# Local attention scores as one wave of 64-row tiles on keys written four times, with new step sequences

## What is computed

```python
q = (hidden @ Wq.T + bq);  k = hidden @ Wk.T + bk;  v = hidden @ Wv.T + bv     # 16 heads of 16 features
scores[t, w] = q[t] . k[w] / sqrt(16)   for |t - w| <= 64, else -inf
ctx = softmax(scores) @ v;  out = ctx @ Wo.T + bo
x = layernorm(x + out)
```

## Time and profile before

| | us |
|---|---|
| Median of 3 runs | 922.75 (920.75 to 925.92) |
| The profiled execution | 927.65 |
| Its span, first to last instruction | 925.9 |
| Mean granted clock of TensorE | 0.951 |

### The profile page before, as it was taken

The page is one execution under the profiler, slowest core; times in us unless marked ns, Lnnn a source line. Parts: engine busy times, 40 slices in busy tenths (PEclk is TensorE's granted clock), DMA queues, the critical chain, the costliest instruction groups (busy, mean ns, idle before and its releaser), DMA issues.

```text
span 925.9 us, 21096 instructions
## 1 busy us (share of the span) xinstructions
PE 851.3 (92%) x8219; PEld 651.1 (70%) x8219; DVE 641.0 (69%) x1941; ACT 491.0 (53%) x1509; POOL 359.3 (39%) x592
## 2 busy tenths in 40 slices
PE   8989999999778999999987899999988899999992
PEld 5557787676657887766766788776776688776771
DVE  5264986785557786686576679577767778668575
ACT  3144455675545544676554445576555554577653
POOL 0377223016747313106574422303674622201555
PEclk9999999999888999998988799998989999999996
DMA  7890000002423100001341200000322200000001
GB/s 212 248 342 30 1 2 1 2 19 61 158 94 111 36 2 1 2 2 52 129 149 57 88 2 2 1 3 26 108 103 95 110 11 2 1 2 2 1 1 36
DMA packets 22800, 53.37 MB, mean 58 GB/s; under 512 B 3512, under 2 KB 9404, under 8 KB 22700
## 3 DMA queue, kind: packets, MB, share of 16 engines
q1 hardware_dynamic: 22700, 52.02, 16.9%
HBM read 48.71 MB, written 3.31 MB: 56 GB/s over the span
## 4 chain that ended last, share of the span: by engine, by line
PE 64%; DVE 10%; POOL 10%; ACT 5%; SPq 4%; DMA 4%; issue 3%; DVEq 0%; ACTq 0%; POOLq 0%
PE psum L430 11%; PE psum L435 10%; PE psum L472 8%; PE psum L619 7%; PE psum L643 5%; PE psum L634 5%; PE psum L626 3%; PE psum L458 2%; DMA out<-xplus 2%; POOL rstd L1190 2%; POOL xplus L1197 2%; SPq L1288 2%; ACT x L701 2%; PE psum L534 2%; DVE bn L935 2%
## 5 line engine op out<-in xcount | busy, mean ns | idle before, releaser
L701 ACT ACTIVATE x<-res,ez,rstd 100x256 f32<-100x256 f32 x160 | 87.3, 595 | 68.8 <-POOL ez L1193 68.2
L472 PE MATMUL psum<-eT,ctx 128*128 128x100 f32 x768 | 109.3, 303 | 11.8 <-ACT eT L695 6.7
L472 PEld LDWEIGHTS psum<-eT,ctx 128*128 128x128 f32 x768 | 104.6, 218 | 13.9 <-ACT eT L695 7.2
L1188 POOL TENSOR_SCALAR ve<-mv 100x2 f32<-100x2 f32 x96 | 21.9, 228 | 216.6 <-DVE mv L938 213.6
L803 ACT ACTIVATE work<-psum,mx 100x100 f32<-100x100 f32 x256 | 67.3, 354 | 43.5 <-DVE mx L1099 42.9
L458 PE MATMUL psum<-ctxT,qT 128*100 128x361 f32 x256 | 83.7, 469 | 1.9 <-ACT qT L717 1.6
L695 ACT ACTIVATE eT<-psum 100x400 f32<-100x400 f32 (+3 forms) x128 | 61.2, 486 | 43.6 <-PE psum L465 24.9
L1190 POOL TENSOR_TENSOR rstd<-ve,minus_half 100x2 f32<-100x2 f32 x96 | 75.5, 786 | 8.0
L1172 POOL TENSOR_TENSOR kT<-cell,kT 100x722 f32<-100x722 f32 x12 | 20.6, 1717 | 147.8 <-ACT cell L675 147.8
L619 PE MATMUL psum<-kT,qT 32*100 32x200 f32 x512 | 74.2, 373 | 1.3 <-DVE aT L1111 0.4
L935 DVE BATCH_NORM_STATS2 bn<-res 100x6 f32<-100x256 f32 x192 | 71.3, 414 | 0.0
(11 more groups left out here) (235 smaller groups left out, 2025.9 us busy)
## 6 DMA issues: line engine op xcount, KB each, us to landing
ctx<-in_ctx SPq DMA_DIRECT2D x16, 768.0 KB, 6.8
ctxT<-in_ctxT SPq DMA_DIRECT2D x16, 722.0 KB, 4.8
cell<-in_cell SPq DMA_DIRECT2D x12, 282.0 KB
seq<-in_seq SPq DMA_DIRECT2D x12, 282.0 KB
x<-in_x SPq DMA_DIRECT2D x16, 200.0 KB
out<-xplus SPq DMA_DIRECT2D x16, 200.0 KB
eT<-agent_rows SPq DMA_DIRECT2D x12, 200.0 KB
work<-in_x SPq DMA_DIRECT2D x4, 400.0 KB
```

The costliest lines, as they stand in the source:

```text
L472: last = e.matmul(bk[b][:, c * S:(c + 1) * S], s.ctx[:, b, j, c * P:(c + 1) * P], s.pT[:, b, j, :], start=j == 0, stop=j == S2C - 1)
L701: e.activation(dst[0:S, b, :], s.res[0:S, b, :], ACT.Identity, scale=s.rstd[:, b:b + 1], bias=s.shift[:, b:b + 1]).then_inc(*act.up(f"x{b}"))
```

## The change

The local scores come in one wave of two 64-row tiles: 64 rows hold four heads, and the keys are stored four times, each with the features of one of the four heads kept by a new constant mask `heads` (128x4). One product of 64 rows against 400 columns fills a bank. VectorE writes the keys of each round i by an instruction of its own (128x400), four to a stage instead of two. As four copies need twice the room, the keys of rounds 0 and 2 lie in `kT`, those of round 1 in `work`, those of round 3 in `res`, both of which hold nothing else at that time. The semaphore step `hs` and the yield between the waves are gone; v1 waits for the last of the four keys. The constant is loaded by one more transfer.

The strings in `ORDER` are new for all engines. PE's has 836 letters instead of 900 (four fewer for each of the 16 local stages); DVE (786), ACT (752), POOL (236) and SP (52) have as many as before, in another order. SP's string is shown below.

```diff
-    "local": "xT q k v0 v1 " + " ".join(f"hs{i} s{i} tra{i} trb{i} av{i}" for i in range(NB * NC)) + " out0 out1",
+    "local": "xT q k v0 v1 " + " ".join(f"s{i} tra{i} trb{i} av{i}" for i in range(NB * NC)) + " out0 out1",
...
-    "local": "k0 k1 v1 " + " ".join(f"ma{i} mb{i} eT{i} rd{i} aT{i}" for i in range(NB * NC)) + " " + NORM,
+    "local": "k0 k1 k2 k3 v1 " + " ".join(f"ma{i} mb{i} eT{i} rd{i} aT{i}" for i in range(NB * NC)) + " " + NORM,
...
+        heads = sb("heads", [P, 4])
...
+                k_rows = s.kT[:, :, :, :].rearrange("p j c t -> p (j c t)")
+                s.keys = [k_rows[:, 0:4 * S], s.work[:, HQ * S:HQ * S + 4 * S], k_rows[:, 4 * S:8 * S],
+                          s.res[:, :, :].rearrange("p b d -> p (b d)")[:, 0:4 * S]]
...
-                e.wait_ge(*dve("k1", t))
+                e.wait_ge(*dve("k3", t))
                 tokens(bk[0][0:S, 0:D], batch(s.xT, 1), W["a_v"]).then_inc(*pe.up("v1"))
...
-                    for wave in range(2):
-                        if wave:
-
-                            e.wait_ge(*pe(f"hs{i}", t))
-                        for g in range(2):
-                            r = 32 * (2 * g + wave)
-                            last = e.matmul(bk[g][0:S, wave * T:(wave + 1) * T], s.qT[r:r + 32, c, b * S:(b + 1) * S],
-                                            s.kT[r:r + 32, :, c, b * S:(b + 1) * S], start=wave == 0, stop=False,
-                                            skip_group_check=True)
-                        if wave == 0:
-                            last.then_inc(*pe.up(f"hs{i}"))
-                            yield
+                    for g in range(2):
+                        r = 64 * g
+                        e.matmul(bk[g][0:S, 0:4 * S], s.qT[r:r + 64, c, b * S:(b + 1) * S], s.keys[i][r:r + 64, :],
+                                 start=True, stop=False, skip_group_check=True)
...
-                for h in range(NC):
-
-                    e.scalar_tensor_tensor(s.kT[:, :, h, :], bk[0][:, h * T:(h + 1) * T].unsqueeze(1).to_broadcast([P, 2, T]),
-                                           cols["a_bk"][:, h:h + 1], own[:, :].unsqueeze(2).to_broadcast([P, 2, T]),
-                                           ALU.add, ALU.mult).then_inc(*dve.up(f"k{h}"))
+                for i in range(NB * NC):
+                    b, h = divmod(i, NC)
+                    at_ = h * T + b * S
+                    e.scalar_tensor_tensor(s.keys[i].rearrange("p (h k) -> p h k", h=4),
+                                           bk[0][:, at_:at_ + S].unsqueeze(1).to_broadcast([P, 4, S]), cols["a_bk"][:, h:h + 1],
+                                           heads[:, :].unsqueeze(2).to_broadcast([P, 4, S]), ALU.add, ALU.mult).then_inc(
+                        *dve.up(f"k{i}"))
...
     "SP": (
-        "ABCDAABBCACBDCDDABCADABACBBACCDDDBCADABCABCBDDCDCBAD"),
+        "ABCDAAABABDBCCDCDBCADABCBACADBDCDBCDABAABBCCDCDDBCAD"),
...
+        "heads": (np.arange(P)[:, None] // DH % 4 == np.arange(4)).astype(np.float32),
```

More of the change, by code:

```diff
@@ L1320, in sync_first @@
                 e.dma_start(rows[n][:, :], ins[n].to_broadcast([P, D])).then_inc(ld_const, 16)
-            for n, tile in (("ident_b", ident_b), ("before", before), ("own", own), ("band_w", band_w), ("band_x", band_x)):
+            for n, tile in (("ident_b", ident_b), ("before", before), ("own", own), ("heads", heads), ("band_w", band_w),
+                            ("band_x", band_x)):
                 e.dma_start(tile[:, :], ins[n]).then_inc(ld_const, 16)
@@ L1390 @@
     "PE": (
[L1391 to L1399, removed]
-    "DVE": (
[L1401 to L1408, removed]
@@ L1409 @@
-    "ACT": (
[L1410 to L1417, removed]
+        "ABCDAABCBCABDACAAADAABCDBBCBBBCACDCDDCDDDAAABCAABCBABADBCBCADBACBACBDDCBCABDDCAACDBDACDABBAADCBADCCB"
@@ new lines @@
+        "ACDBCBDABCDACDBCADBCADBCBDCBCAADBCDACBCABCDDABACDBABDACCDBDCBADACDAADDBAABAADABCDBBBBCBABCCADCCCCDCD"
+        "ABABDADDDDDAACBABACABABBBCDBDBCABCACACACDCCDCBADABDBDBDCBADADDBACCACDBABCDBCDDCABDCBCDAADCBCDADABDAB"
+        "CABADCCBDCACBBDBDCCDAABCDABCDBADCBCDABADACBBADDCBADACBCADABBCDDABCBCDACACDBABAACADADBABDCBBBDCBBCADA"
+        "DCCDCCCCBADBADADDDAADBCACBAABABBBBDCBCABDCACACACCDCCDAABDBDBBADCADDDDBABCCBCADCBCADBDDCBDCABDCAACDDC"
+        "BADABDBCABADACCBDCABCBDABCDADCBCDABCDBADCBCDABADABCBADDCBAADBCADCBABCDBCDABCACDACDBAABACAADDABDCBBBB"
@@ new lines @@
+        "CBBDCACADCCDCCCDBABADDADDDADAABACBCAABBBBCDACDBCABBCACCADCCCADABDBADBBACDDDDDBABCCCABDCBACDBDDBACCDB"
+        "DCADABCDACDABAADCBBADCCBACDBBCDACBDADCBCDABCBADDBCDCBAADACBBDADCBADACBCADCABBCDDBDCABCACDABCBADDAAAC"
+        "DAACDBCBBADBBACCDBBCCDCDCDDDDDBBCCDD"),
+    "DVE": (
+        "ABCCBACDDADAAACBBAACBDBACDBAACDCBDCDDBCBACDABCDAAAABABADBBACCBBBBACBCDCDCCCBDDCADDDDAACADBABDACBBCCC"
+        "ABADBACDBBCADCDCBAABDCBBCDACCDADCBAABCDBABCCDABADDACBCDBDBDDAAACDACADABBBAABBDDCBCACBCABDCDCBDAADCBC"
+        "ADDACABDBCBADABADBACBCDCBABCACCBDDAACDABBCACDAADDBBADCBDBCBDBACCDBDCCCCBDCDDADDDACDAABABADCBBCCCBAAD"
+        "BCADBBCDDACCBAADBDCBABDADCBAADCCBDABCAABDADBCBCDBCBCADADCACDAADCBBBADDDBAACBBCABCABCCDCDBDBACDAACDDD"
+        "CAABBABCDAABBADCBCCDBCBAACCBDCDAAACDBCADABADDBBDACBDCBDBBCACBDDCCCCBDCDADDDDADCAABBADACBBCACACBDBDCA"
+        "BBCDDACCBADABDCBABDADCAABDCBACDBBAADCDABCBCDCBBCDAADCACDCAADABBBADBADDBCCBCABCABDCDCBDACABDDADCACAAB"
+        "BCBADDADACBCDBCBAABCBCCABDCADACDBCAAABDDDABBDCDBBCBDBACCBDCCDCCBDDCADDDDACADABAABDCBBACBCACDBACDBBCD"
+        "DACBCAADBDCBBADDACBAADCCBDABBCADCDABCDCBDCBCAADDCADADAADABBABCCBCBBACDBDCDCBDDDCBCDDCD"),
@@ new lines @@
+    "ACT": (
+        "AABCBAACACBDCABAADABCCBDBDACBCBDADCDDDBACBACDDABAABABCCBCABDABBDCACDCBACABDDACDBDABACBDACCCDBBDBCADC"
+        "AACDBBDBCDCCDAABBABCCDCDAAADBBCBCADCDADABAADDABABDACABBCBBABCABCCDCADCBCBCDADADADBDAADBCCDAABBAABCBD"
+        "DCBBCBABDCACCDCACACDCBBDADDCDBADBDCABDACADCBDABCBDDCABCCDBACADBDCADBDAABCACDBCDDBCBBCCADADACBBDDDCBC"
+        "AAACBBDBDDAACCCABABBDDADACBCACABAABCADDBBDABCBBBAACCDCDACDCDDBABCCADBADABADCADCBAABCDABBDCBBABCBCACD"
+        "CCADCABCACBDDDDCDBDBAACBADDCBADCDCBABDCBDDCABCACADDBCADBDBCAADABCCDBCBDAABCDCDCABBDDBCCDAACABBDDDBAA"
+        "ACCBBABCDDADCACCBAABAABDABACBDCDBBBAACBCDCACDCDCBBDCADABADDAACADBDCABAABCDDBBCBBACBABCDCCCDCADCABADB"
+        "CDADCDCBBDADADBACDCBBDCABDDCBACDABCCDABDCBDADAACBDCABCDCBBDABCCDADCABBBDDCDCACAABBDDBDAACACCBBDDBDCA"
+        "ACCAABBADDAADCABBCCCAABBDABCDCBDDCBCBDDDDCCBDDACDBCD"),
@@ L1418 @@
     "POOL": (
-        "AABCBADCBCDADBCDABACBAADCBDCDAAABBABBCCCBAACADCDDBBADBADACBCCBBDCDDCACDDBDCADBACAABDCCDBDAAABBABBCBC"
-        "CACADACDDBABDBADACBCCBBDCDADCCDDBDCADBACBBADCACDAAABBBACBDBCCACAADCDDBDABBADACBCBCDBCDDCACDDBDCADBAA"
-        "CBDCBDCADABACBCACBAADDABDBBCCCDDDBCD"),
+        "ABACBDABCCDADBCDABAAACBDCCBDAABABBADCBCBCADAACCDDBDABBADABCCCBBDDCDCACDDBDCADBACBDCAADCBDAABABBACBBC"
+        "CCADAADDCDBABBADABCBCCDBCDDACCDBDDCADBACBDCAADBDACABABABCBCBCAAADCDCDDBABBDAACBCBCDBDCADCCDDBDCADBAC"
@@ L1422 @@
+        "ABDCDDBAACBABCCBAAADCDDBBABCCCDDDBCD"),
     "SP": (
-        "ABCDAABBCACBDCDDABCADABACBBACCDDDBCADABCABCBDDCDCBAD"),
+        "ABCDAAABABDBCCDCDBCADABCBACADBDCDBCDABAABBCCDCDDBCAD"),
 }
@@ L1432 @@
 LD_W0, LD_WK, LD_C = 16 * 3, 16 * 3, 16 * (5 + len(EARLY_ROWS) + len(COLVECS) - 1 + 2)
-LD_FIRST, LD_CONST = 16 * 4, 16 * (7 + 2 + 6)
+LD_FIRST, LD_CONST = 16 * 4, 16 * (7 + 2 + 7)
 def constants():
```

## The result

The changed kernel takes 918.63 us (median of 20 runs, 911.11 to 925.24) against 923.52 us for the kernel before (20 runs): ratio 0.9942, interval 0.9925 to 0.9959. The ratio leaves out the few executions that ran clearly slower, such as one of 2682.62 us of the kernel before. That is 5.4 us faster where 15.3 were forecast, inside the wide range (897 to 925) but outside the forecast's own (900 to 916). The profiled execution has a span of 917.6 us, 8.3 less than before.

A forecast was written before the change was run, and what follows sets the result against it. The prediction took PE to bound the local stretches, with chains of other engines and transfers between them. Scores save 17.3 us, keys cost 2, so 15.3 off the 922.75 us median gives 907.5; range 897 to 925.

The forecast's parts named there:

- The new wave, 0.85 us, and 17.3 us of PE's time: Local scores on PE: one 0.85 us wave replaces two of 0.515, saving 0.27 us at 64 places, 17.3 us.
- Two tiles at once: Local scores on PE: the two 64-row tiles run concurrently, as four matmuls at L583 took 0.60 us, not 0.86.
- rival (d): Local scores: the two 64-row tiles of 400 columns take turns, adding 25 us, to 947.5 us; chance 0.04.
- The keys, 2 us: VectorE's two extra key writes a stage, 17.6 us in all, are covered by PE; 2 us taken off for them.
- Rival (b): VectorE's longer key step delays v1 or other streams' maxima, eating up the saving: 923 us, no change; chance 0.13.
- What a step takes of PE's time is worth its full length: Local stretches: PE itself is the bound, busy 312.5 of 320 us, so the 17.3 us saved there counts in full.
- a sign of being wrong: The prediction is wrong if PE waits in the local stretches where it had no waits, or if the turns grow.
- I have no row that prices the new sequences: All engines: new sequences reorder the same operations; their effect, of either sign, lies at the turns and was left to rivals.
- rival (c): New SP order puts one more 7.1 us store wait on each of three turns, adding 21.3: 928.8 us; chance 0.14.

The follow-up runs named there:

- e3: Changed kernel with only two of the four key writes a stage (output differs from the reference): 919.85 us, ratio 0.994 to the kernel before.
- e13: Changed kernel with two second-turn stores earlier in SP's string and only two of the four key writes (output differs from the reference): 904.92 us, ratio 0.981.
- e4: Kernel before with two more 128x400 key writes in each local stage, v1 waiting for the last of the four: 928.4 us, ratio 1.0035.
- e1: Changed kernel (one wave, four keys) on the old sequences, PE's string only losing the 64 first-wave letters: 917.52 us, ratio 0.991 to the kernel before.
- e6: Changed kernel with the output normalized into an idle part of work, so POOL no longer waits for the store: 908.29 us, ratio 0.9833.
- e7: Kernel before with the output normalized into an idle part of work, so POOL's addition no longer waits for the store: 918.02 us, ratio 0.9933.
- e8: Changed kernel with scores against 200 of the 400 columns (output differs from the reference): 906.0 us, ratio 0.9807 to the kernel before.
- e11: Changed kernel with two second-turn stores earlier in SP's string and scores against 200 of 400 columns (output differs from the reference): 894.44 us, ratio 0.9686.
- e14: Kernel before on the new sequences, old waves side by side, with two second-turn stores earlier in SP's string: 937.96 us, ratio 1.0176.
- e10: One wave on the old sequences, with stores of the first and third turns moved earlier in SP's string: 907.86 us, ratio 0.983 to the kernel before.
- e5: Changed kernel with the second turn's stores of streams A and B moved earlier in SP's string, ahead of context loads: 905.84 us, ratio 0.9805.
- e9: Kernel before with the second turn's part of SP's string as in the changed kernel, two stores behind more loads: 933.58 us, ratio 1.0113.
- e2: Kernel before on the new sequences, each pair of old waves side by side: 956.41 us, ratio 1.0317 to the kernel before.

## Why the forecast was wrong

- **The new wave, 0.85 us, and 17.3 us of PE's time: right.** 0.849 us measured, PE's busy time 16.7 us less (a little of that is the clock, 0.956 granted against 0.951).
- **"Two tiles at once": right**, no sign of rival (d), which would have made the wave 1.4 us or more. The prediction gave rival (d)'s sum also to the case that the factors are 4 and 2; that doesn't follow, since a factor of 2 for 64 rows is the two tiles at once that were measured.
- **The keys, 2 us: too much.** No difference in the changed kernel, with and without the late stores (e3, e13); 3 us in the old one (e4), where PE waits for the last key (2.6 us in e1). Rival (b) is out.
- **"What a step takes of PE's time is worth its full length": this step failed.** It was read from PE's busy share, 312 of 320 us, and its few waits. The edit on the old sequences brought 8.3 us of 17 (e1), or 11 if the keys' 3 us there are added back; with the store's landing taken out on both sides, 0.9833 against 0.9933, 9 us of 17 (e6 against e7, sequences changed too); and 21 us of PE's work brought 12.5 and 11 us (e8, e11). So the term was mis-sized, by a factor of about two in most of these comparisons; each is known to some 3 to 5 us, and e14 speaks for a smaller factor. One place where the time went is shown, and the prediction had named it as a sign of being wrong: PE's idle time in the stretches rose from 5.8 to 10.8 us (10.4 in e1, 10.2 without the extra keys in e3, and from 10.1 to 14.0 when still more work was taken off in e11). That fits a PE that with less work arrives earlier and waits for others, VectorE's `aT` among them; which wait took how much wasn't tried. In the profiled executions 13 to 15 us of the 17 show in the stretches (13.7 from before to after, 15 to e1, 13 from e7 to e10), and the rest is given back in start and gaps; but these differ by 2 to 5 us between single executions (the start is 140.1 us in the changed kernel and 142.0 with the stores ahead, where SP's string differs only later; the third gap is 140.3 us in e1 and 135.2 before, at granted clocks of 0.93 and 0.96), so that how the rest splits stays open.
- **"I have no row that prices the new sequences": the other step that failed, by omission.** It was rival (c), with the right mechanism, put at nothing in the sum and given too low a chance; it priced one wait of 7.1 us in each of three turns, and there came two, of 8.3 and 9.1, in one turn. There was a row: the store's landing is 7.1 us where it stands behind contexts, and the new SP string, read step by step, shows A's store of the second turn behind two more of SP's steps (C's contexts, B's x) and B's behind three (C's x, A's masks, D's contexts). Measured, those two places are worth 12.7 us (e5), and 10 us in the mirror (e9). That is more than the 6.6 us by which the second gap grew, but those compare two different sequences. On the same sequences, with and without the late stores (the changed kernel and e5), that gap differs by 11.7 us: PE is idle for 10.5 us less, and runs some 10 us less at the 1.2 GHz level (granted clock 0.98 instead of 0.94 over the gap). One turn was hit, not three, and the waits of the first and third turn left the chain in exchange.

Together: half of the saving, 8 to 9 us, on the old sequences. The new ones change this by about +3 us: 12.7 lost at two stores, and so some 10 gained elsewhere, most of it probably the waits of before that are gone (moving their stores brings 7 us in e10). Each term of this sum is known to some 3 to 5 us. The forecast of 907.5 us is met by the changed kernel with two letters of SP's string moved (905.84), but partly for another reason than its sum.

## What to carry to other kernels

A busy share of 98% and few waits don't make PE's time worth its full length, since waits that the work covered come to light when it goes: price it by an experiment that only takes work away, before the sum is made. When queues are written out by hand, read a new transfer order step by step against the one before, and ask of each store which later write waits for its landing and how many bytes stand ahead of it. Here that reading was worth 12.7 us, and the edit itself 8 on the old sequences.

## What was not expected of the hardware

- A store of 200 KB took 8.3 and 9.1 us from issue to landing behind 1.9 and 2.5 MB of loads that were issued within 2.4 us ahead of it. Issued 0.4 us ahead of contexts instead, with only an x load just ahead of it, it took 3.6 us (279.19 in the kernel before). Issued 3 us ahead of them (469.02 against 472.00 in e5), it held up nothing on the chain.
- PE fell to the 1.2 GHz level for over 40 us while its busy share was 98 to 99% (e14, and e2 as well). What it did before: rows of short float32 steps with the two waves side by side, each pair with 0.14 us of waiting in the middle. Whether that waiting or something else brought it down wasn't tried.
